# A routed MLP kernel on one core: table work moved behind the first group, class loads ahead of transposes, idle matmuls in TensorE's waits

## What is computed

```python
out_nr = gelu(x @ w1_nr + b1_nr) @ w2_nr + b2_nr          # condition 0
out_tsr = gelu(x @ w1_tsr + b1_tsr) @ w2_tsr + b2_tsr     # condition 1
h = gelu(x @ w1_sr + b1_sr)                               # condition 2, hidden 512
h = gelu(h @ w2_sr + b2_sr)
out_sr = h @ w3_sr + b3_sr
out = where(c == 0, out_nr, where(c == 1, out_tsr, where(c == 2, out_sr, 0)))
y = x + out
return (y - mean(y)) * rsqrt(var(y) + 1e-5) * gamma + beta
```

## Time and profile before

| | us |
|---|---|
| median of 3 runs | 107.52 (107.29, 107.52, 108.08) |
| profiled execution | 107.55 |
| its span | 105.8 |

### The profile page before, as it was taken

How to read it: one execution, slowest core, us unless ns; L and a number is a source line. 1 busy time by engine, 2 the same in 40 slices (tenths; PEclk the granted TensorE clock), 3 DMA queues, 4 the chain that set the end, 5 groups by cost and what they waited for, 6 DMA issues and landing times.

```text
span 105.8 us, 1727 instructions
## 1 busy us (share of the span) xinstructions
PE 84.9 (80%) x500; PEld 73.5 (69%) x500; DVE 78.3 (74%) x210; ACT 61.3 (58%) x101; POOL 62.2 (59%) x80
## 2 busy tenths in 40 slices
PE   0259969999999999999999999999999999600000
PEld 0157548868888987899899898997998989500000
DVE  5678996764275394365998989799988899999800
ACT  0685318997788204897796794968958853400000
POOL 7527900008877704002496989787987898697600
PEclk9999999999999999999999999999999999997555
DMA  0795996000089993000000403004013040050470
GB/s 1 277 321 149 288 314 244 6 0 0 12 291 280 350 412 150 0 0 6 0 6 0 198 9 152 28 6 198 0 50 155 0 194 11 12 198 9 189 235 12
DMA packets 5349, 12.60 MB, mean 119 GB/s; under 512 B 608, under 2 KB 2672, under 8 KB 5328
## 3 DMA queue, kind: packets, MB, share of 16 engines
q0 software_dynamic: 2672, 9.57, 24.6%
q1 hardware_dynamic: 2636, 2.76, 7.9%
q10 hardware_dynamic: 20, 0.01, 0.0%
HBM read 8.14 MB, written 4.46 MB: 119 GB/s over the span
## 4 chain that ended last, share of the span: by engine, by line
PE 66%; DVE 16%; DMA 4%; issue 4%; POOL 2%; ACT 2%; DVEq 0%; ACTq 0%; POOLq 0%
PE ps_f L1020 19%; PE ps_a L958 8%; PE ps_a L963 8%; PE ps_a L959 8%; PE ps_x L935 6%; DMA xs<-x_dram,load_idx 4%; PE ps_f L1007 3%; PE ps_b L1081 2%; PE ps_b L1080 2%; PE ps_b L1082 2%; DVE ps_f L810 2%; DVE xs L817 2%; DVE stats L852 1%; PE ps_a L1080 1%; DVE stats L766 1%
## 5 line engine op out<-in xcount | busy, mean ns | idle before, releaser
L457 POOL TENSOR_TENSOR xs<-xs,gamma_b 128x768 f32<-128x768 f32 (+1 forms) x7 | 12.4, 1772 | 8.1 <-ACT xs L544 7.9
L958 PE MATMUL ps_a<-x_hi,w_lo 128*128 128x512 f32 (+1 forms) x40 | 16.1, 404 | 0.8 <-ACT x_hi L577 0.8
L1020 PE MATMUL ps_f<-wf_lo,f_hi 128*128 x64 | 15.9, 282 | 0.0
L1020 PE MATMUL ps_f<-wf_hi,f_hi 128*128 x64 | 15.9, 282 | 0.0
L540 ACT ACTIVATE f_hi<-ps_a,bias_cols 128x512 fp32r<-128x512 f32 (+1 forms) x16 | 10.6, 662 | 9.1 <-PE ps_a L1082 4.8
L959 PE MATMUL ps_a<-x_hi,w_hi 128*128 128x512 f32 (+1 forms) x40 | 15.2, 383 | 0.0
L541 ACT ACTIVATE ps_a<-ps_a,bias_cols 128x512 f32<-128x512 f32 (+1 forms) x22 | 14.0, 634 | 0.0
L446 POOL TENSOR_TENSOR rstd<-var_eps,half 128x4 f32<-128x4 f32 (+1 forms) x9 | 9.0, 1001 | 8.0 <-DVE var_eps L783 7.9
L413 POOL DMA_INDIRECT xs<-x_dram,load_idx x10 | 9.6, 964 | 5.7 <-DVE load_idx L687 3.1
L1020 PEld LDWEIGHTS ps_f<-wf_hi,f_hi 128*128 128x128 f32 x64 | 12.0, 188 | 0.7
L462 POOL TENSOR_TENSOR xs<-xs,beta_b 128x768 f32<-128x768 f32 (+1 forms) x7 | 12.3, 1763 | 0.1
(11 more groups left out here) (163 smaller groups left out, 193.1 us busy)
## 6 DMA issues: line engine op xcount, KB each, us to landing
w_raw<-L_cond_w_sr_dram SPq DMA_DIRECT2D x2, 512.0 KB, 4.3
wf_raw<-L_cond_w_sr_dram SPq DMA_DIRECT2D x1, 256.0 KB, 5.0
w_raw<-L_cond_w_tsr_dram SPq DMA_DIRECT2D x1, 256.0 KB, 5.2
w_raw<-L_cond_w_nr_dram SPq DMA_DIRECT2D x1, 256.0 KB, 5.5
wf_raw<-L_cond_w_tsr_dram SPq DMA_DIRECT2D x1, 256.0 KB, 5.6
wf_raw<-L_cond_w_nr_dram SPq DMA_DIRECT2D x1, 256.0 KB, 5.7
xs<-x_dram,load_idx POOLq DMA_INDIRECT x10, 6.1
gamma_b<-L_cond_gamma_dram SPq DMA_DIRECT2D x1, 128.0 KB, 3.7
```

Source lines behind the costliest of these rows:

```text
L457: nc.gpsimd.tensor_tensor(tiles, tiles, spread(gamma_b, n), ALU.mult).then_inc(gam_pool, 1)
L958: nc.tensor.matmul(dst, w1_lo[:, kt, cols], xh[:, kt, :], start=(kt == 0), stop=False)
L1020: return nc.tensor.matmul(ps[:, b, t * H:(t + 1) * H], stationary[:, kt, (2 * b + t) * P:(2 * b + t + 1) * P], weights[:, bass.ds(f_at + k ...
```

## The change

- VectorE: the memsets of `ones2` and `warm_x` come first and signal `warm_ready`. The bias rest becomes `bias_parts()` and the eight instructions behind `bias_cols` become `places()`; both run at the end of VectorE's step 0. `half_rows()` moves from ahead of the steps to step 1.
- TensorE: the three table products become `place_tables()`, in step 1 between the first layer of group 1 and the last layer of group 0. The class load comes ahead of the transposes of group 0. Idle matmuls: 3 ahead of the counts, 4 behind them, 1 behind the row table and 9 ahead of the class load, where there were 10.
- ScalarE: the class load comes ahead of the two pieces of `x_hi`.
- GpSimd: the half group's gather moves from behind the other gathers to step 2.
- `long_second`: the product with `h_lo` comes last in each group of three, and for the fourth k-tile of the first block only that product waits for `h_lo`; the other two wait for the GELU.

```diff
--- before.py
+++ after.py
@@ -156,6 +156,7 @@
         pool_step = sem("pool_step")
         zeroed = sem("zeroed")
         dve_step = sem("dve_step")
+        warm_ready = sem("warm_ready")
         own_done = sem("own_done")
         counts_ps = sem("counts_ps")
         place_done = sem("place_done")
@@ -206,7 +207,8 @@
 
 
         ORDER_CONSTS, CONSTS = 10, 17
-        WARM = 10
+
+        WARM_OWN, WARM_PLACE, WARM_BIAS, WARM_ROWS = 3, 4, 1, 9
 
         EARLY = 3
 
@@ -429,10 +431,6 @@
                                         ).then_inc(wf_lo_done, 1)
             for s in range(EARLY, SLOTS):
                 gather(s)
-            pool.wait_ge(half_idx_done, 1)
-            nc.gpsimd.indirect_dma_start(
-                out=xs_half[:, :, :].rearrange("p t h -> p (t h)"), out_offset=None, in_=half_x_rows,
-                in_offset=bass.IndirectOffsetOnAxis(ap=half_load_idx[:, 0:1], axis=0)).then_inc(half_loaded, 16)
             pool.wait_ge(bcast_in, 16 * 2)
             pool.wait_ge(pool_step, 3)
 
@@ -481,7 +479,15 @@
                     plus_beta(g - 1, POOL_TT)
                     scatter(g - 1, False)
 
+            def gather_half():
+                pool.wait_ge(half_idx_done, 1)
+                nc.gpsimd.indirect_dma_start(
+                    out=xs_half[:, :, :].rearrange("p t h -> p (t h)"), out_offset=None, in_=half_x_rows,
+                    in_offset=bass.IndirectOffsetOnAxis(ap=half_load_idx[:, 0:1], axis=0)).then_inc(half_loaded, 16)
+
             def pool_step_of(s):
+                if s == 2:
+                    gather_half()
                 if s > 0:
                     pool_group(s - 1)
 
@@ -572,12 +578,12 @@
             wf_high(0)
             act.wait_ge(bf_in, 16 * 3)
             nc.scalar.activation(bf_round[:, :], bf_raw[:, :], ACT.Copy).then_inc(bf_rounded, 1)
+            act.wait_ge(bias_done, 1)
+            act.wait_ge(tab_done, 1)
+            cls = load_classes(act, "act_cls")
             for kt in range(KT):
                 act.wait_ge(xT_ready, kt + 1)
                 nc.scalar.activation(x_hi[0][:, kt, :], ps_x[:, kt, :], ACT.Copy).then_inc(x_hi_done, 1)
-            act.wait_ge(bias_done, 1)
-            act.wait_ge(tab_done, 1)
-            cls = load_classes(act, "act_cls")
 
             def act_step(s):
                 f = f_hi[s % 2]
@@ -632,10 +638,10 @@
                 ins.then_inc(dve_step, 1)
                 dve.wait_ge(dve_step, step[0])
 
+            nc.vector.memset(ones2[:, :].bitcast(F32), 1.0)
+            nc.vector.memset(warm_x[:, :].bitcast(F32), 1.0).then_inc(warm_ready, 1)
             nc.vector.memset(zeros[:, :], 0.0)
             nc.vector.memset(bf_parts[:, :].bitcast(F32), 0.0)
-            nc.vector.memset(ones2[:, :].bitcast(F32), 1.0)
-            nc.vector.memset(warm_x[:, :].bitcast(F32), 1.0)
             dve.wait_ge(cond_in, 16)
             chain(nc.vector.tensor_scalar(key[:, :], cond_col[:, :].bitcast(U32), float(NR), None, ALU.min))
             dve.wait_ge(consts, ORDER_CONSTS)
@@ -708,25 +714,32 @@
             nc.vector.tensor_copy(cls_tab[:, :], cls_f[:, :]).then_inc(tab_done, 1)
             dve.wait_ge(rows_t, 1)
             nc.vector.tensor_copy(bias_cols[:, :], bias_pt).then_inc(bias_done, 1)
...
+            def bias_parts():
+                dve.wait_ge(bf_rounded, 1)
+                nc.vector.scalar_tensor_tensor(out=bf_parts[0:2, :], in0=bf_round[:, :].bitcast(F32),
+                                               scalar=minus_row[:, 0:1], in1=bf_raw[:, :], op0=ALU.mult, op1=ALU.add
+                                               ).then_inc(bf_done, 1)
+
+            def places():
+
+                nc.vector.scalar_tensor_tensor(out=place[:, :], in0=base[:, :], scalar=float(PER), in1=rank[:, :],
+                                               op0=ALU.mult, op1=ALU.add).then_inc(dve_step, 1)
+                nc.vector.tensor_scalar(near[:, :], nth[:, :], FAR / 2, None, ALU.is_lt).then_inc(dve_step, 1)
+
...
+                nc.vector.tensor_scalar(at_place[:, PLACES:PLACES + HPER], place_id[:, 0:HPER], half_place[:, 0:1], None,
+                                        ALU.is_equal).then_inc(at_place_done, 1)
+                nc.vector.scalar_tensor_tensor(out=half_row_at[:, :], in0=half_row_place[:, :], scalar=half_place[:, 0:1],
+                                               in1=half_row_val[:, :], op0=ALU.is_equal, op1=ALU.mult
+                                               ).then_inc(half_place_done, 1)
 
             def half_rows():
                 dve.wait_ge(half_rows_ps, 1)
@@ -864,21 +877,17 @@
                 root_and_beta(g, half_tile, xs_half, HTT, u_last)
 
             w_low(0)
-            dve.wait_ge(bf_rounded, 1)
-            nc.vector.scalar_tensor_tensor(out=bf_parts[0:2, :], in0=bf_round[:, :].bitcast(F32),
-                                           scalar=minus_row[:, 0:1], in1=bf_raw[:, :], op0=ALU.mult, op1=ALU.add
-                                           ).then_inc(bf_done, 1)
             for kt in range(KT):
                 dve.wait_ge(x_hi_done, kt + 1)
                 nc.vector.tensor_tensor(x_lo[0][:, kt, :], ps_x[:, kt, :], x_hi[0][:, kt, :].bitcast(F32),
                                         ALU.subtract).then_inc(x_lo_done, 1)
             w_low(1)
             dve.wait_ge(tab_done, 1)
-            half_rows()
             cls = load_classes(dve, "dve_cls")
 
             def norm_part(s):
                 if s == 1:
+                    half_rows()
                     dve.wait_ge(places_ps, 1)
                     nc.vector.tensor_copy(place_tab[:, :, :], places_pt).then_inc(place_tab_done, 1)
                 if s >= 1:
@@ -913,17 +922,29 @@
                 with dve.If(cls[s] < TSR):
                     for m, bank in ((0, ps_a[1]), (1, ps_b)):
                         low(bank[:, 0, :], f[:, m, :], f_l[:, m, :], HID * s + HT + m + 1, 1)
+                if s == 0:
+                    bias_parts()
+                    places()
 
             each_step(dve, cls, dve_step_of, dve_half, final)
 
         @block.tensor
         def _(pe):
+            def keep_busy(n):
+
+                for _ in range(n):
+                    nc.tensor.matmul(ps_f[:, 0, :], ones2[:, :], warm_x[:, :], start=True, stop=True)
+
+            pe.wait_ge(warm_ready, 1)
+            keep_busy(WARM_OWN)
             pe.wait_ge(consts, ORDER_CONSTS)
             pe.wait_ge(own_done, 1)
             nc.tensor.matmul(counts_pt, ones_b[:, :], own[:, :], start=True, stop=True)
             nc.tensor.matmul(ranks_pt, tri[:, :], own[:, :], start=True, stop=True).then_inc(counts_ps, 1)
+            keep_busy(WARM_PLACE)
             pe.wait_ge(place_done, 2)
             nc.tensor.matmul(rows_pt, row_at[:, :], in_slot[:, :], start=True, stop=True).then_inc(rows_ps, 1)
+            keep_busy(WARM_BIAS)
             pe.wait_ge(consts, CONSTS)
             pe.wait_ge(rows_in, 16 * 4)
             nc.tensor.transpose(bias_pt, bias_rows[:, :], ident[0:16, 0:16]).then_inc(rows_t, 1)
@@ -1075,28 +1096,34 @@
                     cols = slice(m * P, (m + 1) * P)
                     pe.wait_ge(low_done, HID * g + 2 + m)
                     for kt in range(HT):
-                        if m == 0 and kt >= 2:
+                        late = m == 0 and kt == HT - 1
+                        if late:
+                            pe.wait_ge(gelu_done, HID * g + kt + 1)
+                        elif m == 0 and kt >= 2:
                             pe.wait_ge(low_done, HID * g + kt + 1)
                         nc.tensor.matmul(dst, w2_lo[:, kt, cols], h_hi[:, kt, :], start=(kt == 0), stop=False)
-                        nc.tensor.matmul(dst, w2_hi[:, kt, cols], h_lo[:, kt, :], start=False, stop=False)
-                        mm = nc.tensor.matmul(dst, w2_hi[:, kt, cols], h_hi[:, kt, :], start=False,
+                        nc.tensor.matmul(dst, w2_hi[:, kt, cols], h_hi[:, kt, :], start=False, stop=False)
+                        if late:
+                            pe.wait_ge(low_done, HID * g + kt + 1)
+                        mm = nc.tensor.matmul(dst, w2_hi[:, kt, cols], h_lo[:, kt, :], start=False,
                                               stop=(kt == HT - 1))
                     mm.then_inc(mm_ready, 1)
 
-
-            for i in range(WARM):
-                nc.tensor.matmul(ps_f[:, 0, :], ones2[:, :], warm_x[:, :], start=True, stop=True)
-            transpose_x(0)
-            pe.wait_ge(at_place_done, 2)
-            nc.tensor.matmul(places_pt[:, 0, :], seq_ones[:, 0:1], at_place[:, :], start=True, stop=True)
-            nc.tensor.matmul(places_pt[:, 1, :], seq_ones[:, 1:2], at_place[:, :], start=True, stop=True
-                             ).then_inc(places_ps, 1)
-            pe.wait_ge(half_place_done, 1)
-            nc.tensor.matmul(half_rows_pt, half_row_at[:, :], seq_ones[:, 1:2], start=True, stop=True
-                             ).then_inc(half_rows_ps, 1)
```

(33 more changed lines are left out.)

9 lines of the change are left out of this document (added).

## The result

| | before | changed |
|---|---|---|
| median | 107.50 us (14 runs, 106.82 to 108.17) | 108.43 us (14 runs, 107.74 to 109.93) |
| ratio to before | | 1.0076, 95% interval 1.004 to 1.0113 |
| span of the profiled execution | 105.8 | 107.5 |
| start of VectorE's last group of instructions in the profile | 99.18 | 100.72 |

What follows compares the result with a forecast made beforehand. TensorE bounds the kernel from 28 to 84 us; before that it waits, with `x_lo` the first stage's gate. Terms -1.57 - 0.10 - 0.33 + 1.55 + 0.60 = +0.15 us gave 107.7 us, range 106.8 to 108.9.

Steps and rivals of the forecast that it cites:

- part 1: First group: `x_lo`, the gate of the first layer, comes earlier; gain 1.57 us, bounds 1.2 and 1.8.
- part 2: Row table before the first gather: idle matmuls may raise the clock, so the gather starts earlier; gain 0.1 us.
- part 3: `long_second`, step 0: TensorE no longer stops for `h_lo` at the fourth k-tile; gain 0.33 us.
- part 4: Step 1, ahead of the fourth block: moved bias rest and `places` delay `h_lo`; loss 1.55 us, bounds 1.2 and 2.7.
- part 5: Step 1, before `last_layer(0)`: table products hold TensorE where it has no gap; loss 0.6 us, bounds 0.4 and 0.8.
- The sum: Whole kernel: all gains and losses together give +0.15 us, 107.7 us; own range 107.2 to 108.1, chance 0.58.
- rival D: First group: idle matmuls don't raise the clock before 11.73 and the class load comes late; 108.3 us, chance 0.09.
- A: After step 0: GpSimd's gathers hold VectorE's small instructions, costing 1.2 us; 108.9 us, chance 0.17.
- B: Step 1: no stall, because VectorE's additions fit into time counted as taken; 106.1 us, chance 0.11.
- C: First group: the array's clock falls while TensorE waits from about 9.5 to 11.73; 1.7 us, 109.4, chance 0.05.

## Why the prediction came out as it did

**The gate of the first layer (part 1): right in kind, half the size.** That `x_lo` and not the class load is the gate is shown by the class loads alone (no shift) and by the VectorE parts back in place (second transposes at 16.07). The gain was 0.83 instead of 1.57. The term that failed is the time of the first four transposes, for which I put 0.44 us and `x_hi` at 12.20. `x_hi` started 0.73 later, which is 0.73 of the 0.74 missing:

```profile
12.93 1.12 ACT L586 ACTIVATE x_hi<-ps_x 128x512 fp32r<-128x512 f32 x2 [3.37 <-PE ps_x L956]
```

Two things are in it. The first 0.25 is a wrong reading. I halved the 0.87 us that eight transposes hold in the chain, but only the starts halve (0.79 us for eight, 25.90 to 26.69), not the last one's way to its end. The rows of before had it: transposes of 1.10 against 1.03 at the full clock leave next to nothing to win, and `x_hi` started 0.70 behind the first of them. In the five other profiles with transposes of 1.06 to 1.09 it started 0.66 to 0.70 behind. The other 0.48 is the clock, which I took to be up: these transposes took 1.64 us, more than the 1.10 of before. Where they took 1.08 (the kernel with VectorE's parts in its waits: `x_hi` at 12.45, second transposes at 14.76) the gain was 1.31, the 1.34 that the forecast gave for no gain in the transposes. The class load behind nine slow idle matmuls cost nothing: the transposes started at 11.78.

**The earlier index (part 2): nothing.** The row table started at 6.21 and took 0.60 us, as in the earlier trace rows (6.21 and 0.59).

**The fourth k-tile (part 3): right.** 0.29 and 0.35 for a forecast of 0.33.

**VectorE's added work (part 4): right.** 1.77 for 1.55, in the place and by the releaser that were named; VectorE's way from `f_lo` to `h_lo` took 4.50 (27.38 to 31.88) for 4.3. The added work is 2.77 for 2.51: the bias rest held VectorE for 1.20 instead of 1.13, and `places` for 1.57 instead of 1.38, with a gather beside it.

**The tables (part 5): 0.90 for 0.60.** The products hold 0.69; I had taken off 0.15 for the last result's way out, and had not added that TensorE loses 0.10 going into them and 0.10 behind them (0.33 for 0.23), as after a stop.

**The sum.** The misses are 0.74, 0.10, 0.04, 0.22 and 0.30, together 1.40, and with the +0.15 they give the +1.55 of the profiled execution. All of them lie on the slow side, so nothing cancelled. That execution is outside the range; the median, +0.93, is inside it but outside the sum's own 107.2 to 108.1. It is next to rival D's 108.3, though D's late class load didn't come: that nearness is chance. The median would fit with the profile if the clock was up in time in some of the executions; both profiles of the changed kernel are of the other kind, so this is argued, not shown. What is shown is each term in the profiles, not why the median is in the range.

**The rivals.** A's mechanism exists, at 0.2 us here and at 2.5 us in the kernel with `places` behind `w_low(0)`. There the held comparison's successor is recorded as started at 11.43 although it was held too, so a recorded start alone doesn't prove that the engine moved on. For the 1.33 us of the earlier trace rows my argument against A holds all the same: `w_low(0)` took its usual 1.21 us from 11.06 and the bias rest followed at 12.19, so the comparison had delayed nothing. The Trainium skill's rule (SBUF — State Buffer, Who interferes with whom) is that GpSimd and a VectorE comparison in its two-port mode exclude each other. No view here shows the mode, but the 2.81 us, which end with GpSimd's subtraction, agree. B didn't come: the stop is there. C, a fall of the clock in a wait, didn't come in the changed kernel, but it did in the kernel with `places` behind `w_low(0)`, where the granted clock was 0.50 after 1.6 us without a product. So the 4.2 us at 1.00 that I held against it were no proof. Most of D's first half came: the idle matmuls didn't raise the clock before 11.73 in this profile.

## What to carry to other kernels

Work taken off one engine's critical stretch has to be put into that engine's waits, not behind its last instruction of a stage: here the same 2.8 us cost 1.77 at the end of step 0 and nothing in two waits of the same engine. Sum what stands between the moved work and the next consumer and compare it with the slack (1.1 us here); it predicted the stop to 0.2 us. Don't halve the time of a group of instructions to get that of half of them: only the distance between their starts divides, and that mistake cost the forecast 0.25 us. Before moving small VectorE instructions, look at what GpSimd does in the new place as well.

## What the hardware showed that I had not expected

- A 64x80 comparison on VectorE stood for 2.81 us beside GpSimd's gather, memsets and subtraction (0.31 us otherwise), and the reverse: GpSimd's third gather took 1.69 us to issue with `w_low(0)` at 9.69 beside it, and 0.94 with `w_low(0)` at 11.06. So it is in all profiles: 1.68 to 1.70 in the eight with the early `w_low(0)`, 0.94 or 0.95 in the five with the late one. Moving `w_low(0)` ahead pushed GpSimd's next work from 10.94 to 11.71.
- Idle matmuls from 1.66 to 11.88 us, with few gaps, left the array at 1.2 GHz in both profiles of the changed kernel and in three more of the eight with that order, while ten that began at 7.2 to 7.3 had it up for the transposes in three of four. That is too few to call one order better. The granted clock read 1.00 throughout.
- After a wait of 1.62 us without a product the granted clock fell from 1.00 to 0.50 in one profile, and its products were then 0.42 us apart instead of 0.23.
- The last stores' way from VectorE's last instructions to the end of the span varied by 1.3 us between profiles, more than most effects measured here.
